# Token scales spread over the channels through DRAM instead of by ones-by-diagonal matmuls

## What is computed

```
mu = jnp.mean(xs, axis=-1, keepdims=True)
var = jnp.mean((xs - mu) ** 2, axis=-1, keepdims=True)
xn = (xs - mu) / jnp.sqrt(var + EPS) * ln_g + ln_b
mid = jax.nn.silu(xn @ fc1_w + fc1_b) @ fc2_w + fc2_b
...
q = q / jnp.linalg.norm(q, axis=-1, keepdims=True)
k = k / jnp.linalg.norm(k, axis=-1, keepdims=True)
attn = jnp.einsum('bhld,bhle->bhde', k, v)
o = 0.5 * v + 1.0 / math.pi * jnp.einsum('bhld,bhde->bhle', q, attn)
o = o / jnp.linalg.norm(o, axis=-1, keepdims=True)
o = o + mid
o = o @ proj_w + proj_b
```

## Time and profile before

| what | us |
|---|---|
| median of 3 runs | 2887.33 |
| lowest and highest of them | 2885.53, 2902.11 |
| the profiled execution | 2895.52 |
| its span, first to last instruction | 2893.7 |
| PE busy | 2779.8 |
| DVE busy | 2027.5 |
| ACT busy | 1177.1 |
| POOL busy | 688.1 |

### The profile page before, as it was taken

How to read it: one execution, slowest core, us unless ns; L and a number is a source line. 1 busy time by engine, 2 the same in 40 slices (tenths; PEclk the granted TensorE clock), 3 DMA queues, 4 the chain that set the end, 5 groups by cost and what they waited for, 6 DMA issues and landing times.

```text
span 2893.7 us, 41252 instructions
## 1 busy us (share of the span) xinstructions
PE 2779.8 (96%) x14930; PEld 2535.6 (88%) x14930; DVE 2027.5 (70%) x2630; ACT 1177.1 (41%) x2040; POOL 688.1 (24%) x211
## 2 busy tenths in 40 slices
PE   6997799999999899999999999999999999999999
PEld 5554699999999799999999899999999899999998
DVE  4786784888887685798888685788898733543443
ACT  3332166344442266344443166344443254333332
POOL 0002043322224044222224044222224033211120
PEclk8998899999999999999999999999999999999999
DMA  5134942133326832133435843133335832111110
GB/s 216 34 89 155 331 122 86 49 113 116 116 95 183 277 116 94 44 103 106 132 113 163 281 131 95 47 100 104 121 127 152 280 111 82 39 39 39 48 39 29
DMA packets 189883, 341.14 MB, mean 118 GB/s; under 512 B 10736, under 2 KB 173424, under 8 KB 186864
## 3 DMA queue, kind: packets, MB, share of 16 engines
q1 hardware_dynamic: 180384, 311.14, 33.3%
q0 software_dynamic: 4480, 19.27, 2.3%
q10 hardware_dynamic: 4816, 8.03, 0.8%
HBM read 234.89 MB, written 103.51 MB: 117 GB/s over the span
## 4 chain that ended last, share of the span: by engine, by line
PE 79%; issue 8%; DMA 6%; DVE 5%; ACT 2%; SPq 1%; POOL 0%; ACTq 0%; DVEq 0%; POOLq 0%
PE bank L748 16%; PE bank L750 16%; PE bank L749 16%; PE bank L787 4%; PE bank L946 4%; PE bank L948 3%; PE bank L947 3%; PE bank L1146 3%; PE bank L968 3%; PE bank L1130 2%; DMA X<-x_scr 2%; PE bank L1097 1%; PE bank L1201 1%; DMA pair_scr<-VT 1%; DMA X0Q<-in_x 1%
## 5 line engine op out<-in xcount | busy, mean ns | idle before, releaser
L1699 ACT ACTIVATE S<-bank,b1p 128x448 f32<-128x448 f32 x336 | 212.1, 631 | 874.8 <-PE bank L750 872.6
L2352 DVE SCALAR_TENSOR_TENSOR AC<-XV,wfold,AC 128x1568 f32<-128x1568 f32 x288 | 529.9, 1845 | 2.7
L748 PE MATMUL bank<-SH,W2H 128*128 128x448 f32 x1008 | 392.9, 390 | 2.8 <-DVE SL L2321 2.8
L750 PE MATMUL bank<-SH,W2L 128*128 128x448 f32 x1008 | 377.1, 374 | 0.0
L749 PE MATMUL bank<-SL,W2H 128*128 128x448 f32 x1008 | 375.7, 373 | 0.0
L748 PE MATMUL bank<-XRH,W1H 128*128 128x448 f32 x1008 | 372.8, 370 | 0.0
L750 PE MATMUL bank<-XRH,W1L 128*128 128x448 f32 x1008 | 369.6, 367 | 0.0
L749 PE MATMUL bank<-XRL,W1H 128*128 128x448 f32 x1008 | 368.7, 366 | 0.0
L666 POOL TENSOR_TENSOR rq<-qn,nhalf 112x32 f32<-112x32 f32 x28 | 181.9, 6495 | 430.5 <-DVE qn L2291 430.5
L658 POOL TENSOR_TENSOR rk<-kn,nhalf 112x24 f32<-112x24 f32 (+1 forms) x56 | 200.8, 3597 | 288.1 <-DVE kn L2113 288.1
L670 POOL TENSOR_TENSOR ro<-on,nhalf 112x32 f32<-112x32 f32 x28 | 179.8, 6421 | 310.3 <-DVE on L2312 310.3
(11 more groups left out here) (236 smaller groups left out, 5397.8 us busy)
## 6 DMA issues: line engine op xcount, KB each, us to landing
X<-x_scr SPq DMA_DIRECT2D x52, 672.0 KB, 5.2
XV<-in_xp SPq DMA_DIRECT2D x36, 870.0 KB, 6.7
XC<-in_xp SPq DMA_DIRECT2D x14, 1682.0 KB, 11.5
CQ<-q_scr SPq DMA_DIRECT2D x28, 672.0 KB, 7.6
CX<-in_x SPq DMA_DIRECT2D x28, 672.0 KB, 5.2
x_scr<-CX SPq DMA_DIRECT2D x28, 672.0 KB, 5.3
V<-v_scr SPq DMA_DIRECT2D x28, 672.0 KB, 4.9
Y<-x_scr SPq DMA_DIRECT2D x28, 672.0 KB, 4.2
```

Source lines behind the costliest of these rows:

```text
L748: mm(o, wh, xh, start=first, stop=False)
L750: return mm(o, wl, xh, start=False, stop=stop)
L1699: fn(S[:, j % 2, :], bank[j % 2][:, 0:T], ACT.Silu, bias=b1p[:, j:j + 1]).then_inc(s["s_s"], 1)
L2352: stt(o, XV[h][:, ky:ky + HR, kx:kx + W], wfold[:, kind, k, 3 * ky + kx:3 * ky + kx + 1], o, ALU.mult, ALU.add).then_inc(s["va"], 1)
```

## The change

The change drops `token_diag` and `spread_r`. In their place ACT issues two DMAs for each tile. `roots_out` waits for rr and writes it, transposed, to a scratch `r_scr` [4, 112] in DRAM. `roots_spread` waits until that has landed and reads the 448 numbers back to each of the 128 partitions of a tile `RB` in SBUF. `scale_x` waits for this read and multiplies X with RB in place of the PSUM bank. PE's waits for the scale in `attend` and `offset_dots`, and one on offset copies ahead of the first tile's `spread_r`, go with it.

```diff
@@ act @@
+                def roots_out(n):
+                    act.wait_ge(s["rr_s"], n + 1)
+                    act.dma_start(r_d.rearrange("u p -> p u"), rr[:, :], allow_slow_non_contiguous=True).then_inc(s["r_st"], 16)
+                def roots_spread(n):
+                    act.wait_ge(s["r_st"], n * 16 + 16)
+                    act.dma_start(RB[:, :], r_d.rearrange("(o u) p -> o (u p)", o=1).to_broadcast([P, T])).then_inc(s["r_ld"], 16)
@@ act, keys and values @@
                         values_out(n, t, u)
+                        if (t, u) == (STRIPS - 1, 2):
+                            roots_out(n0)
+                        if (t, u) == (STRIPS - 1, 3):
+                            roots_spread(n0)
@@ act, tile @@
                     silu(n, 6)
                     if not last:
+                        roots_out(n + 1)
                         query_out(n + 1, 1)
                         query_out(n + 1, 2)
+                        roots_spread(n + 1)
                     silu(n, 7)
@@ pe @@
-                        if (t, u) == (STRIPS - 1, 3):
-                            if nxt:
-                                pe.wait_ge(s["oc_ev"], (b + 2) * (2 * KC))
-                            spread_r(n0, 7)
...
                     elif step == 4:
                         pe.wait_ge(s["ml"], n * KC)
-                        spread_r(n, 6)
                         query_norms(n, 7)
@@ dve @@
-                    if not last:
-                        token_diag(n + 1)
...
-            def scale_x(n, p):
-                dve.wait_ge(s["rb_mm"], n + 1)
-                tt(X[:, :, :], X[:, :, :], bank[p][:, 0:T].unsqueeze(1).to_broadcast([P, KC, T]), ALU.mult).then_inc(s["xsr"], 1)
+            def scale_x(n):
+                dve.wait_ge(s["r_ld"], n * 16 + 16)
+                tt(X[:, :, :], X[:, :, :], RB[:, :].unsqueeze(1).to_broadcast([P, KC, T]), ALU.mult).then_inc(s["xsr"], 1)
```

More of the change, by code:

```diff
@@ L84, in build @@
     v1_d = scratch("v1_scr", (L, C))
+    r_d = scratch("r_scr", (SUB, TS))
     x1_v = x1_d.rearrange("b (k p) l -> b p k l", p=P)
@@ L202, in build @@
         rve, rr = sb("rve", [TS, SUB], at=at), sb("rr", [TS, SUB], at=at)
-        rh, rl = sb("rh", [TS, SUB], F32R, at=at), sb("rl", [TS, SUB], at=at)
         qn, rq = sb("qn", [TS, SUB * NH1], at=at), sb("rq", [TS, SUB * NH1], at=at)
@@ L207, in build @@
         VS = sb("VS", [TK, 2, C], at=list(at))
-        DH, DL = sb("DH", [TS, SUB, TS], F32R, at=at), sb("DL", [TS, SUB, TS], F32R, at=at)
+        RB = sb("RB", [P, T], at=list(at))
+        at[0] += 2 * C * 4
         S = sb("S", [P, 2, T], at=at)
-        o1r = sb("o1r", [TS, P], F32R, at=at)
         assert at[0] <= stats_at
@@ L260, in build @@
             wo_ld kxs kxh kxl k_mm v_mm k_sq k_ev v_ev k_red k_rs k_hat v1_st0 v1_st1 at_mm ab_s
-            x_ld v_ld y_ld y_st xh xl xt_mm bn_s ag_s rve_s rr_s rh_s rl_s dg rb_mm xsr xrh xrl
+            x_ld v_ld y_ld y_st xh xl xt_mm bn_s ag_s rve_s rr_s r_st r_ld xsr xrh xrl
             q_mm q_ev qq qs_mm qn_s rq_s qa_mm o_sc o_mx o_sq o_red ro_s o_fin ot_mm
@@ L972, in image @@
                 n0 = b * STRIPS
[L974 to L980, removed]
                 def bank7_free(keys, offsets):
@@ L1025, in offset_dots @@
                     pe.wait_ge(s["gelu"], (b + 2) * KC)
-                    pe.wait_ge(s["xsr"], n0 + 1)
                     for t in range(STRIPS):
@@ L1137, in attend @@
                         pe.wait_ge(s["q_ev"], n * KC + KC)
-                    if u == 1:
-                        pe.wait_ge(s["xsr"], n + 1)
                     if u == 2:
@@ L2191, in keys_values @@
                         key_scale(n - 1, 1 - t % 2, 1)
-                    if last:
-                        first_tile("diag")
                     if nxt:
@@ L2205, in keys_values @@
                             dve.wait_ge(s["ktp"], KTB + (b + 1) * (2 * KC))
-                        dve.memset(f(o1r[:, :]), 1.0)
                         for u in range(2):
@@ L2228, in run @@
                         token_var(n)
-                    elif what == "diag":
-                        token_diag(n)
                     elif what == "scale":
-                        scale_x(n, 7)
+                        scale_x(n)
                     elif what == "split":
@@ L2416, in tile @@
                     if not last:
-                        scale_x(n + 1, 6)
+                        scale_x(n + 1)
                         query_norm(n + 1, 7)
```

9 lines of the change are left out of this document (removed).

## The result

The changed kernel takes 2904.62 us (median of 20 runs, 2890.02 to 2916.54), the kernel before 2887.02 (20 runs, 2879.94 to 2902.11). The ratio is 1.005, with a 95% interval of 1.0034 to 1.0066. The forecast was 2854 and its range ended at 2872. Beside other kernels on another chip the changed kernel gave 1.0069 (1.0043 to 1.0095).

What follows compares the result with a forecast made beforehand. PE, busy 96% of the span, was taken as the bound. Terms -23.2 (spread), -2.4 (DVE) and -8 (clock) gave -34 from the median 2887.3: 2853, rounded up to 2854 us; range 2838 to 2872.

Steps and rivals of the forecast that it cites:

- The spread on PE, -23.2: Spread matmuls removed from PE in 28 tiles at 0.83 us each, saved in full: 23.2 us less.
- DVE, -2.4: Diagonals dropped on DVE: PE's 0.8 us wait for V goes in tile 0 of images 0 to 2, ML's wait not growing.
- The clock, -8: Shorter run of small matmuls on PE: 5 of 19 falls to 1.2 GHz go, at 1.6 us each, 8 us less.
- The write, 3 us taken: ACT's write of 448 4-byte pieces to DRAM lands in 3 us, so ACT doesn't wait for it: cost 0.
- below 6.8: Regular tiles: a write landing up to 6.8 us after issue costs PE nothing; the rows' 1.9 and 6.5 lie below.
- the room of the first tile at 3.5 us: Each image's first tile: 3.5 us from the write's issue to the end of the last values' copy, called enough at 3.
- ACT, the wait, at 0: A late write makes ACT stand before SiLU 7 and MH; idle time up to PE's wait for ML covers it: cost 0.
- nothing on PE waits for X before the next tile's fc1: DVE's product of X with RB: any difference from reading SBUF instead of PSUM is covered, so none was taken.
- The read, 2.1 to 3 taken, 3.8 allowed: First tile of each image: the read into RB lands in 2.1 to 3 us, within 3.8 us before PE wants XRL: cost 0.
- The 11 us kept for the range: First tiles: a read of 6.5 us would cost 2.7 us in each of four images; kept for the range, not the sum.
- The write is late: Rival: write lands beyond 6.8 us, ACT stands, PE waits before the norms, 24 us per us beyond, kernel slower; chance 0.12.
- Only the direct part: Rival: clock falls as often or slightly more, or first tiles' reads 2 us late: 2861 to 2869 us; chance 0.25.

Runs made afterwards that it cites:

- first_mm: Changed kernel, but each image's first tile spreads by diagonals and matmuls as before, the 24 others by the two DMAs: 2860.77 us, ratio 0.9899 to the kernel before.
- write_twice: first_mm with a second write of the same size to another scratch, the read waiting for both: 2896.08 us, ratio 1.0014 to the kernel before.
- wide64: Changed kernel with the write's 448 pieces 64 bytes apart and RB filled from a broadcast input row; write lands in 1.8 us, run time not used.

## Why the prediction was wrong, by its steps

*The spread on PE, -23.2.* Right as such: `first_mm` is 0.87 us a tile shorter. Not foreseen was that dropping two small tiles shifts fc1's operands, at 0.3 us a tile: +9 of it came back.

*DVE, -2.4.* The wait for V went, as said. ML's wait grew by 0.17 us in each of three tiles, which I had excluded: -1.9.

*The clock, -8.* Seven of the 19 falls went in the changed kernel's profile, at 1.6 us some 11 us. The direction holds in the profiles of all kernels with the change in the regular tiles: 11 to 17 falls, 18 in `write_twice`.

*The write, 3 us taken.* This step failed. It landed in 6.4 us. The bounds from the earlier trace rows (1.9 to 6.5) were passed by nine of 28, among them three of the four first tiles (up to 7.5). In the regular tiles the sum needed only "below 6.8". That nearly held: three of 24 landed beyond, and PE waited for ML in none but tile 0. But I had put the room of the first tile at 3.5 us, wrote "enough at 3", and did not carry the upper bound, 6.5, to that place. By my own rows it would have been 3.0 us late. Measured in image 0: 483.0 less 479.6, 3.4 us.

*ACT, the wait, at 0.* I followed the late MH to ML and the norms, where the room is 7.1 us, and no further. Behind ML on DVE stand X and `query_norm`, and the attention on PE waits for what comes of them: 3.2 us in 8 tiles. My "nothing on PE waits for X before the next tile's fc1" overlooked DVE's order.

*The read, 2.1 to 3 taken, 3.8 allowed.* It took 4.5 there, 0.7 too much. The earlier trace rows are stores to DRAM, while this one reads from it. 3.4 + 0.7 is 4.1; PE waited 4.04 us.

*The 11 us kept for the range.* They were the read's upper bound alone, and only the waiting. With the write it is 16 us, and behind three of the four waits the clock was lower than before, which in sum costs as much again. The falls behind the small matmuls stood in my working, at 1.6 us each; a fall behind a stall had no price.

*The sum.* In profile terms: -23.2, -1.9, -11, +16.3 of waiting, +15 of clock, +9 of shifted operands, +3.2 for QQ are +7. PE's waits for VS (the sampled values, DVE) are 3.1 us less in the changed kernel's profile, 4.8 in place of 7.9; no term of mine has them, and in the other kernels they are 4.6 to 15.3. That leaves +4, and the spans differ by +1.1. The clock's two terms are the weak ones: the granted clock of the whole span is 0.961 in both profiles, so over the whole span it cost the same, where -11 and +15 would leave +4.

*The rivals.* "The write is late" had the right suspect and the wrong place: its price was in the 24 regular tiles, from 6.8 us on, and decided at 9.1. The Trainium skill (DMA: Bandwidth & Descriptors, Rules for kernel authors) speaks against the non-contiguous write, and that was borne out: 6.4 us, and 1.4 when rearranged. Its reason, one descriptor for each element, is not the whole of it here, since `wide64` has as many 4-byte elements and lands in 1.8. "Only the direct part" counted the late first tiles at "2 us"; they were 4, and eight with the clock.

## What to carry to other kernels

Give every place that uses a transfer its own room, and hold the upper bound of an unknown landing against the smallest of them; a bound that is harmless 24 times can decide the other four. Follow a late transfer through every engine whose order it shifts, not only to the first wait. Price a stall of a saturated TensorE at about twice its length here, once for itself and once for the clock behind it. Don't write a small result in 4-byte neighbours: keep a partition's numbers in one piece or the pieces apart, issue it early, and compare a matmul's spacing after an unrelated tile is dropped.

## What the runs showed of the hardware

- A store of 448 pieces of 4 bytes to DRAM lands in 6.4 us when they are neighbours, 2.4 us 16 bytes apart, 1.8 us 64 bytes apart; the same numbers as 112 pieces of 16 bytes land in 1.4 us.
- A broadcast read of 1792 bytes to 128 partitions takes 3.2 us, but 5.3 us from a row that 4-byte pieces have only just filled, and still 4.2 to 5.6 us up to 1.3 us later.
- TensorE, filled with useless matmuls for 4.18 us of its wait, runs at 2.4 GHz behind it (0.21 us a matmul of 448 columns). Idle for 4.04 us, it runs at 1.2 GHz (0.37 us).
- A move of fc1's moving operands by 64 bytes in SBUF changes the spacing of its matmuls from 0.200 to 0.203 us.
- A VectorE product of 128x1344 takes 2576 ns when it walks in pieces of 112 and reads one operand at a stride of four, 1554 ns without.
